# A 14-layer transformer kernel on one core: shared score banks in causal attention, one copy of q, split shift transfers, new order tables

## The reference

```python
# level 1 "ffn": causal attention, then a mixture of experts (twice)
scores = jnp.einsum('bqhd,bkhd->bhqk', q, k) * scale
scores = jnp.where(causal[None, None], scores, -jnp.inf)
attn = jax.nn.softmax(scores, axis=-1)
# level 1 "attn": linear attention with a causal mask, q and k of unit length
# level 2 "attn": softmax attention inside blocks of 32 tokens, causal
# level 3 "attn": softmax attention over all 512 tokens
# level 3 "layer" (4 times): local attention, then
h = shift_token(x)          # half of the features from the token before
h = (h - mu) / jnp.sqrt(var + 1e-05) * lg + lb
a, g = jnp.split(h @ w1 + b1, 2, axis=-1)
x = x + (a * gelu(g)) @ w2 + b2
```

## Time and profile before

| what | value |
|---|---|
| median of 3 runs | 3526.99 us (3520.63 to 3535.27) |
| the profiled execution | 3510.88 us |
| its span, first to last instruction | 3509.0 us |
| instructions in the span | 64853 |
| busy PE, DVE, ACT, POOL | 2800.5, 2270.1, 1778.4, 906.9 us |
| mean granted TensorE clock | 0.868 of full speed |

### The profile page before, as it was taken

The page is one execution under the profiler, slowest core; times in us unless marked ns, Lnnn a source line. Parts: engine busy times, 40 slices in busy tenths (PEclk is TensorE's granted clock), DMA queues, the critical chain, the costliest instruction groups (busy, mean ns, idle before and its releaser), DMA issues. The chain is left out here.

```text
span 3509.0 us, 64853 instructions
## 1 busy us (share of the span) xinstructions
PE 2800.5 (80%) x24849; PEld 1787.8 (51%) x24849; DVE 2270.1 (65%) x5496; ACT 1778.4 (51%) x4408; POOL 906.9 (26%) x875
## 2 busy tenths in 40 slices
PE   5856687888875589997777888889887888899875
PEld 3545455544443344456655776555553333556553
DVE  4655566678774567865466445777777767787752
ACT  2333452655622255552356434667665677666642
POOL 1010000111335211111232114545431113454430
PEclk7856786899977699998899989899999999999987
DMA  3423310000000000025610465010100000010000
GB/s 108 188 41 58 59 44 1 1 1 1 1 1 1 1 1 1 1 94 181 230 59 1 139 208 184 15 24 15 24 15 2 1 1 11 13 24 15 20 23 9
DMA packets 136365, 159.41 MB, mean 45 GB/s; under 512 B 84469, under 2 KB 111349, under 8 KB 134522
## 3 DMA queue, kind: packets, MB, share of 16 engines
...
q0 software_dynamic: 2048, 4.20, 0.4%
...
## 5 line engine op out<-in xcount | busy, mean ns | idle before, releaser
L1051 DVE TENSOR_REDUCE nm<-ps 128x1 f32<-128x512 f32 (+4 forms) x832 | 442.6, 563 | 103.4 <-PE ps L972 59.6
L1094 ACT ACTIVATE core<-ps 128x512 f32<-128x512 f32 (+3 forms) x832 | 376.7, 510 | 125.9 <-PE ps L1003 86.4
L274 POOL TENSOR_TENSOR rstd<-ve,weights 128x4 f32<-128x4 f32 x80 | 81.0, 1013 | 1170.0 <-DVE ve L251 1169.5
L427 ACT COPY hand<-ps 64x512 bf16<-64x512 bf16 x448 | 259.8, 580 | 172.1 <-PE ps L459 132.4
L969 PE MATMUL ps<-hand 128*128 128x128 bf16 (+3 forms) x1024 | 296.7, 328 | 60.1 <-DVE nm L1051 33.2
L1000 PE MATMUL ps<-hand 128*128 128x512 bf16 (+3 forms) x1024 | 271.2, 307 | 19.4 <-ACT hand L427 10.1
L1922 POOL TENSOR_TENSOR pre<-pre,sin 128x512 f32<-128x512 f32 x128 | 221.8, 1753 | 244.2 <-ACT pre L1891 227.8
L2038 ACT ACTIVATE core<-ps,nm 128x128 f32<-128x128 f32 x512 | 181.9, 374 | 127.7 <-DVE nm L2053 127.2
L1691 PE MATMUL ps<-hand 128*128 128x128 f32 x1408 | 202.2, 304 | 42.6 <-DMA hand<-in_experts 42.5
L1927 POOL TENSOR_TENSOR ss<-ss,weights 128x16 f32<-128x16 f32 x64 | 195.4, 3054 | 118.0 <-DVE ss L1942 116.4
L1850 PE MATMUL ps<-weights,pre 128*128 128x512 f32 x384 | 209.2, 643 | 18.9 <-ACT pre L1894 18.8
...
## 6 DMA issues: line engine op xcount, KB each, us to landing
...
core<-shear SPq DMA_DIRECT2D x256, 32.0 KB, 1.9
...
```

The lines of the kernel that those rows point to most:

```text
L427: ins = copy(a.QX[64 * e:64 * e + 64, q_slot(2 * pair + e), :], src[64 * e:64 * e + 64, :])
L1051: nc.vector.tensor_reduce(nm_of(h, qts), src, AX.X, ALU.max, negate=True).then_inc(negmax, 1)
L1094: nc.scalar.activation(prob8[:, i % PROBS, 0:L - q0], m.ps[:, RING[at % NR], 0:L - q0], ACT.Exp).then_inc(ring_out, 1)
```

## The change

1. `attend8`, causal form: units that need few columns share a bank. For maxima, the two heads of a pair share a unit in tile 0 (2x128 columns) and one in tile 1 (2x256), tiles 2 and 3 stay alone: 12 units a group of four heads instead of 16, 48 in all. For exponentials, tiles 0 and 1 stay alone, tile 2 takes two heads (2x256) and tile 3 all four (4x128): 11 a group, 44 in all. One matmul adds the mask to all heads of a unit.
2. Level 1, 2 and 3 attention (`once`) keep q and k of a pair in one tile of 128x1024, copied in one piece; a head is read by its 64 rows (`half_rows`), with no zeros. `clear_q` moves to the pre part of level 1 ffn, which still has the zeroed form.
3. The shift of 127 partitions becomes one of 112 and one of 15.
4. All tables of `ORDERS` are other ones.

```diff
+def half_rows(a, h):
+    rows = slice(64 * (h % 2), 64 * (h % 2) + 64)
+    return a.QK[rows, h // 2, 0:L], a.QK[rows, h // 2, L:2 * L]
...
 def turn_stacks(...):      # take()
         eng.wait_ge(lane.filled, f + pair + 1)
+        if once:
+            copy(a.QK[:, pair, :], lane.atb).then_inc(lane.taken, 1)
+            return
         copy_q(copy, a, pair, lane.atb[:, 0:L])
         copy(a.KX[:, pair, :], lane.atb[:, L:2 * L]).then_inc(lane.taken, 1)
...
     elif kind == CAUSAL:
-        first = [([qt], (qt + 1) * P) for qt in range(NT)]
-        second = [([kt], kt * P) for kt in range(NT)]
+        first = []
+        for c in range(2):
+            first += [[(2 * c + e, qt, 0, (qt + 1) * P) for e in range(2)] for qt in range(2)]
+            first += [[(2 * c + e, qt, 0, (qt + 1) * P)] for qt in range(2, NT) for e in range(2)]
+        second = [[(j, kt, kt * P, L)] for kt in range(2) for j in range(4)]
+        second += [[(j, 2, 2 * P, L) for j in (2 * c, 2 * c + 1)] for c in range(2)]
+        second += [[(j, 3, 3 * P, L) for j in range(4)]]
...
         def take_q(g, n):
+            if kind == CAUSAL:
+                copy_q(...)          # two copies of 64x512, as before
+            else:
+                nc.scalar.copy(a.QK[:, 2 * g + n, 0:L], m.psb[:, RING[at % NR], 0:L]).then_inc(ring_out, 1)
...
 def l1_ffn_pre(nc, m, lane, a, b, l):
+    cleared = clear_q(nc, m, lane, a)
...
 def rope_attn_pre(nc, m, lane, a, b, weight, row, interleaved):
-    cleared = clear_q(nc, m, lane, a)
...
     def shift_sync(sp):
-        sp.dma_start(s.h[1:P, :, half:D], y[0:P - 1, :, half:D]).then_inc(moved, 16)
+        sp.dma_start(s.h[1:113, :, half:D], y[0:112, :, half:D]).then_inc(moved, 16)
+        sp.dma_start(s.h[113:P, :, half:D], y[112:P - 1, :, half:D]).then_inc(moved, 16)
         sp.dma_start(s.h[0:1, 1:NT, half:D], y[P - 1:P, 0:NT - 1, half:D]).then_inc(moved, 16)
...
-     "scalar": "b1a1c1a1b1a2b1a1b1a2b1a2b1a5c1a3c1b2a9b1a1b1a7b1a7b1a7b1a18",
+     "scalar": "c1b1a1b1a3c1b1a3c1a3b1a1b1a1b1a7b3a2b1a3b1a5b1a4b1a13",
```

More of the change, by code:

```diff
@@ L444, in clear_q, with turn_stacks @@
     return cleared, 1
-def turn_stacks(nc, m, lane, a, stkk, ready, cleared=None):
+def turn_stacks(nc, m, lane, a, stkk, ready, cleared=None, once=False):
     f = lane.fills(8)
@@ L933, in first_unit, with width, done_by @@
         g, r = divmod(i, N1)
-        pair, r = divmod(r, 2 * len(first))
-        u, e = divmod(r, 2)
-        return 4 * g + 2 * pair + e, first[u]
+        return [(4 * g + j, qt, lo, nk) for j, qt, lo, nk in first[r]]
     def second_unit(i):
         g, r = divmod(i, N2)
-        u, j = divmod(r, 4)
-        return 4 * g + j, second[u]
+        return [(4 * g + j, kt, s, z) for j, kt, s, z in second[r]]
+    def width(unit):
+        return sum(z - s for _, _, s, z in unit)
+    def done_by(i):
+        g, r = divmod(i, N2)
+        return NW * g + min(w for w in range(NW) if r <= weighed[w]) + 1
     def ring_at(i):
@@ L952, in attend8, with nm_of @@
         "scores", "negmax", "max_split", "ring_in", "ring_out", "av", "o_out", "pstep"))
-    def nm_of(h, qts):
-        return m.nm[:, h * NT + qts[0]:h * NT + qts[-1] + 1]
+    def nm_of(unit):
+        at, step = unit[0][0] * NT + unit[0][1], NT if len(unit) > 1 and unit[0][1] == unit[1][1] else 1
+        return m.nm[:, at:at + (len(unit) - 1) * step + 1:step]
     def tensor(pe):
         def score(i):
-            h, (qts, nk) = first_unit(i)
-            q, k = score_rows(a, h)
+            unit = first_unit(i)
             if i >= NS:
@@ L986, in shifted_score @@
         def shifted_score(i):
-            h, (kts, q0) = second_unit(i)
-            q, k = score_rows(a, h)
+            unit = second_unit(i)
             at = ring_at(i)
@@ L1025, in tensor @@
             score(i)
+            given += 1
         yield LEAD
@@ L1028, in tensor @@
         turn_q(0, 1)
-        for i in range(total):
+        for i in range(total2):
             yield LEAD + i
@@ L1035, in tensor @@
             shifted_score(i)
-            if LEAD + i < total:
-                score(LEAD + i)
-            if i >= 6 and i % 4 == 2:
-                weigh(i // 4 - 1)
-        yield LEAD + total
-        weigh(total // 4 - 1)
+            while given < min(total1, LEAD + (i + 1) * N1 // N2):
+                score(given)
+                given += 1
+            while ahead and ahead[0] // NW * N2 + weighed[ahead[0] % NW] + 3 <= i:
+                weigh(ahead.pop(0))
+        yield LEAD + total2
+        for f in ahead:
+            weigh(f)
     def vector(dve):
-        for i in range(GROUPS * N1):
-            yield i + 0.5
-            h, (qts, nk) = first_unit(i)
+        for i in range(total1):
+            yield i + 0.5 if i < LEAD else LEAD + (i - LEAD + 1) * N2 / N1 + 0.5
+            unit = first_unit(i)
             dve.wait_ge(scores, i + 1)
-            src = m.ps[:, SCORES[i % NS], 0:len(qts) * nk]
-            if len(qts) > 1:
-                src = src.rearrange("p (a b) -> p a b", a=len(qts))
-            nc.vector.tensor_reduce(nm_of(h, qts), src, AX.X, ALU.max, negate=True).then_inc(negmax, 1)
+            src = m.ps[:, SCORES[i % NS], 0:len(unit) * unit[0][3]]
+            if len(unit) > 1:
+                src = src.rearrange("p (a b) -> p a b", a=len(unit))
+            nc.vector.tensor_reduce(nm_of(unit), src, AX.X, ALU.max, negate=True).then_inc(negmax, 1)
     def gpsimd(pool):
@@ L1444, in l1_attn_pre @@
     stacked = stack_parts(nc, m, lane, s.raw_heads, a.stkq, s.stkk, s.res, (normed, 1))
-    turned = turn_stacks(nc, m, lane, a, s.stkk, stacked)
+    turned = turn_stacks(nc, m, lane, a, s.stkk, stacked, once=True)
     turn_tok(nc, m, lane, s.raw[:, :, 0:D], a.hT, turned)
@@ L1759, in rope_attn_pre @@
     stacked = stack_parts(nc, m, lane, s.raw_heads, a.stkq, s.stkk, s.res, roped)
-    turn_stacks(nc, m, lane, a, s.stkk, stacked, cleared)
+    turn_stacks(nc, m, lane, a, s.stkk, stacked, once=True)
 def l2_attn_pre(nc, m, lane, a, b, l):
@@ new lines @@
+    {"tensor": "b1a4b1a11b1a7b3",
+     "vector": "b4c1a4b1a1b5a2b1a1b3a1b1a3",
+     "scalar": "a2b1a3b1a6b3",
+     "gpsimd": "c1b2",
+     "sync": "a12b1d1a1"},
+    {"tensor": "b1a3b1a6b1a12b1a1b2",
+     "vector": "b4c1a2b3a1b2a1b2a1b2a1b1a1b1a5",
+     "scalar": "b1a2b1a9b3",
+     "gpsimd": "c1b2",
+     "sync": "a8b1a5"},
+    {"tensor": "b2a1b1a2b1a1b1a11b1a1b1a1b1a1b1a1b1a1b1a2b2",
+     "vector": "b4a1c1a2b3a1b2a1b2a1b2a1b2a1b1a1b1a2b1a1b1",
+     "scalar": "b2a1b1a1b1a1b1a3b1a1b2a1b1a1b1a1b1a1b1",
+     "gpsimd": "b1c1b5",
+     "sync": "a1d1a12"},
```

354 lines of the change are left out of this document (176 added, 178 removed).

## The result

The changed kernel took 3358.31 us (median of 4 runs, 3352.47 to 3360.87) against 3523.81 us of the kernel before on the same occasions: a ratio of 0.952, 95% interval 0.950 to 0.955. The forecast was 3382 us, a gain of 145 us; the gain is 166 us by the medians and 168 by the ratio. Its profiled execution took 3352.47 us with a span of 3350.7 us, 158 us less than that of before.

A forecast was written before the change was run, and what follows sets the result against it. No engine was taken as full: slots are chains of hand-overs, where only work in the chain pays. Terms 64 + 6 + 40 + 15 + 18 - 3 + 5 = 145 us took 3527 to 3382 us; range 3315 to 3448.

The forecast's parts named there:

- Shift: Slots 37 to 44 and 49 to 56: splitting the transfer shortens DVE's wait, 64 us faster, bounds 0 and 89.
- SP's order in slots 53 and 54: SP's queue: the copy of v no longer issues late behind the store, 6 us faster, bounds 0 and 8.7.
- One copy: turn_stacks copies q and k as one 128x1024 piece: 40 us; q copied once in core, slots 44 to 47: 15 us.
- Banks: Causal slots 12 to 15 and 20 to 23: shared units cost DVE and ACT less, 18 us faster, bounds 0 and 46.
- The second rival: Causal slots fall by more than the work they lose, as hand-overs are saved too: 69 us more, 3313 us; chance 0.10.
- Clears: POOL's clear moved ahead of a step in slots 11 to 14 and 19 to 22: 3 us lost, bounds 0 and 14.
- Table loads: Slot 7: 14 loads on ACT become 4, 5 us faster, bounds 2 and 8.
- Slots of only new tables: Slots 0 to 6, 8 to 10, 24 to 26, 32 to 36 and 48: 0, by up to 10 us either way.
- the sign that I had named for being wrong: One of the signs: more than 30 us coming from slots to which the prediction gave nothing.
- The first: Most slots: freed time turns into other waits, only what stands alone pays, 55 us, so 3472 us; chance 0.13.
- The third: Shift: the transfer of 112 partitions is no shorter, so the 64 us go, 3446 us; chance 0.04.
- The fourth: Causal cores: shared units stall DVE; at 20 us a slot the time would be 3560 us; chance 0.03.

The follow-up runs named there:

- e2: The kernel before with only the new order tables, in all slots but 12 to 15 and 20 to 23: ratio 0.993, 26 us faster.
- e1: The kernel before with only the shift of 127 partitions split into 112 and 15, old orders: ratio 0.982, 65 us faster.
- e3: The kernel before with only q and k of a pair in one copy, read by 64 rows, and the clear moved: ratio 1.006, 20 us slower.
- e4: The kernel before with only the shared banks of the causal form and new tables in slots 12 to 15 and 20 to 23: ratio 0.992.
- e7: The changed kernel with level 2 and 3 attention's score matmuls reading all 128 rows (scores not of one head): ratio 0.938, 3300 us.
- e9: The kernel before with one copy of q and k, level 2 and 3 score matmuls reading 128 rows (both heads added): ratio 0.991, 31 us faster.
- e10: The changed kernel with old tables in 14 slots and no clear in slots 11 to 14: ratio 0.948, 3325 us.

## Why the prediction was right, and where it was not

The time and its sign were right, by a sum in which the parts were right in mechanism but for one, the copies in the attention slots. That the total came out so close is luck in part: what this one lost (44 us short of the forecast in slots 27 to 31 and 44 to 47, without slot 44's shift) was made up for by 61 us in slots that I had left at zero.

- **Shift.** Right. 64 us taken, 65 measured alone. In the changed kernel the split carries 88 to 98 us, because the new orders would lose 22 us in its slots without it. I had seen that the wait stood earlier, but counted it as less cover only for the gain, not as a loss of the orders that the split pays back. That the second issue stands until the pieces of the first are taken off one by one is argued; the runs show that it takes 6.47 us behind 127 partitions and 0.94 behind 112.
- **SP's order in slots 53 and 54.** Right in kind, a little small. The issue no longer stands behind the store. The orders alone (e2) gave 3.4 us in the two slots; the split alone (e1) gave 14.2, and the changed kernel 19.2, 5.0 more than the split, for 6 forecast.
- **One copy.** The durations were right to 2 ns, and slots 16 to 18 gave 17.2 us for 16 (14.7 by the copy alone, e3). Slot 15 gave 6.5 for 4, but hardly by the copy: that alone gave 0.9 there, and the banks alone 3.5 (e4). In slots 27 to 31 and 44 to 47 the sum failed: 32 us forecast, 12 us lost. With 128 rows there is a gain, as e7 shows (-23.5 and -26.0 us in these groups against before, the shift in slot 44 included), but the 64 rows cost 61 us over both. (My upper bound of 23 for slots 44 to 47 was added up too low: 4 x 4.6 and 3 x 5.3 make 34.) In the part on the copies I named the form "read by 64 rows" nowhere as a cost: the matmuls are as many, and at the high clock as long (0.39 us for four of 128 rows, 0.40 for four of 64), so I took them as equal.
- **Banks.** Right in mechanism; the size was 18 forecast, 24 measured in the same seven slots, 26 alone in eight. The second rival (69 us more) did not come.
- **Clears.** Right. 3 us forecast, 3.0 by the moved clear alone in slots 11 and 19 (e3). The changed kernel lost 6.6 there, but the new tables without the moved clear lost 4.4 already (e2). In the causal slots no loss is shown.
- **Table loads.** 5 forecast, 3.3 measured (4.4 in e2). ACT's busy time in the slot fell from 36.83 to 23.84 us, by 13.0 us, of which ten loads of 1.283 are 12.8. A drain would be idle time, and there is none: an activation of line 752 or 1285 that has its input starts 0.01 us behind its load (as at 419.35 + 1.28 and 420.64).
- **Slots of only new tables.** "0, by up to 10 either way" failed: 61 us. This was the sign that I had named for being wrong, more than 30 us from slots to which I gave nothing. The order was compared at three places only. 36 us of it are slots 3 to 6, where DVE's waits for the core's transfers fell from 24.9 to 6.1 us, and 25 the other slots, which no run takes apart; e2 shows that both come with the tables (34.7 and 28.6 us).
- **The rivals.** The first (freed time turns into other waits) is false for the shift; in slots 44 to 47 the copies gave 0.4 us in the old orders (e9), which fits it, but at a lower clock than before. The third, no gain from 112 partitions, is false. The fourth, stalls in the causal cores, is false.

What stays open is why fewer rows bring the clock down, why slots 45 and 46 have a clock of 0.87 in e9 with 128 rows, and why slots at the edge, 44 and 47 above all, take the one clock or the other when a distant slot changes (e10). The clock is also higher in the changed kernel in slots 3 to 6 (0.59 to 0.77 in slot 5). It does not look like the cause of the gain there: with the old tables slot 6 took 62.0 to 63.0 us in seven runs at clocks from 0.55 to 0.67.
